# Attention weights times V: one 128-column load of V's two halves in place of two 64-column loads

## What is computed

```python
def _layer(x, wqkv, qs, ksc, wo, lg, lb, w1, b1, w2, b2):
    q, k, v = split(shift_token(x) @ wqkv, 3)          # to 8 heads of 64
    q, k = rotary_xpos(l2norm(q) * qs, l2norm(k) * ksc)
    sim = einsum('bhwid,bhwjd->bhwij', 8 * q, look_around(k))
    attn = softmax(where(mask, -big, sim))
    o = einsum('bhwij,bhwjd->bhwid', attn, look_around(v))
    x = x + o @ wo
    h = layernorm(shift_token(x)) * lg + lb
    a, g = split(h @ w1 + b1, 2)
    return x + (a * gelu(g)) @ w2 + b2
```

## Time and profile before

| what | value |
|---|---|
| median of 3 executions | 3410.75 us (3410.06 to 3413.91) |
| the profiled execution, its own time | 3413.96 us |
| its span, first to last instruction | 3412.1 us |
| mean granted clock of TensorE | 0.977 |
| TensorE matmuls busy / weight loads busy | 95% / 77% of the span |
| VectorE / ScalarE / GpSimd busy | 52% / 43% / 25% |

### The profile page before, as it was taken

The page is one execution under the profiler, slowest core; times in us unless marked ns, Lnnn a source line. Parts: engine busy times, 40 slices in busy tenths (PEclk is TensorE's granted clock), DMA queues, the critical chain, the costliest instruction groups (busy, mean ns, idle before and its releaser), DMA issues. The chain is left out here.

```text
span 3412.1 us, 53427 instructions
## 1 busy us (share of the span) xinstructions
PE 3227.8 (95%) x19624; PEld 2640.0 (77%) x19624; DVE 1765.4 (52%) x3662; ACT 1461.4 (43%) x2957; POOL 841.7 (25%) x1472
## 2 busy tenths in 40 slices
PE   8986999999996999999995999999996999999999
PEld 7975888888875777888774788888885777777777
DVE  4544666666665334434333666666666433334333
ACT  1114777777772111111112777777775211111111
POOL 0005444544436000000002444544543400000000
PEclk9998999999998999999997999999998999999999
DMA  4222111111114111011113111111112311111110
GB/s 140 81 84 90 63 63 60 57 63 60 56 52 121 62 62 56 26 49 62 60 58 138 50 43 49 63 63 60 57 50 81 90 56 62 62 62 62 62 62 32
DMA packets 166889, 224.21 MB, mean 66 GB/s; under 512 B 25017, under 2 KB 94777, under 8 KB 166377
## 3 DMA queue, kind: packets, MB, share of 16 engines
q1 hardware_dynamic: 148152, 201.91, 17.9%
q10 hardware_dynamic: 18480, 18.88, 1.7%
HBM read 130.55 MB, written 60.83 MB: 56 GB/s over the span
## 5 line engine op out<-in xcount | busy, mean ns | idle before, releaser
L308 PE MATMUL bank<-f_hT_hi,f_w_hi 128*128 128x512 f32 (+1 forms) x1408 | 559.5, 397 | 14.7 <-ACT f_hT_hi L973 14.7
L310 PE MATMUL bank<-f_hT_hi,f_w_lo 128*128 128x512 f32 (+1 forms) x1408 | 557.0, 396 | 0.0
L309 PE MATMUL bank<-f_hT_lo,f_w_hi 128*128 128x512 f32 (+1 forms) x1408 | 556.2, 395 | 0.0
L989 ACT ACTIVATE f_gate<-bank,f_b 128x512 f32<-128x512 f32 (+1 forms) x176 | 121.1, 688 | 1004.2 <-PE bank L310 1004.2
L1304 DVE SCALAR_TENSOR_TENSOR f_uraw<-bank,f_b,f_gate 128x512 f32<-128x512 f32 (+1 forms) x176 | 132.1, 750 | 715.6 <-ACT f_gate L989 715.4
L901 ACT ACTIVATE a_P<-a_S,a_bias 128x384 f32<-128x384 f32 x512 | 311.1, 609 | 245.7 <-DVE a_bias L1155 245.7
L1155 DVE CUSTOM_DVE_ANT_0 a_S<-bank,a_masks,a_q 128x384 f32<-128x384 f32 x512 | 295.2, 613 | 61.6 <-issue 45.3
L308 PEld LDWEIGHTS bank<-f_hT_hi,f_w_hi 128*128 128x128 f32 (+1 forms) x1408 | 260.5, 185 | 79.4 <-ACT f_hT_hi L973 15.4
L308 PE MATMUL bank<-a_PT_hi,a_V_hi 128*64 128x128 f32 x1536 | 305.2, 233 | 16.6 <-DVE a_PT_lo L1165 16.6
L310 PEld LDWEIGHTS bank<-f_hT_hi,f_w_lo 128*128 128x128 f32 (+1 forms) x1408 | 260.9, 185 | 67.5
L309 PEld LDWEIGHTS bank<-f_hT_lo,f_w_hi 128*128 128x128 f32 (+1 forms) x1408 | 261.0, 185 | 66.3
(11 more groups left out here) (166 smaller groups left out, 6959.7 us busy)
## 6 DMA issues: line engine op xcount, KB each, us to landing
a_h<-x_layer_in SPq DMA_DIRECT2D x128, 128.0 KB, 2.2
a_res<-x_layer_in SPq DMA_DIRECT2D x64, 256.0 KB, 2.9
x_after_attention<-out_tiles SPq DMA_DIRECT2D x64, 256.0 KB, 2.0
f_h<-x_after_attention ACTq DMA_DIRECT2D x32, 512.0 KB, 4.2
f_res<-x_after_attention SPq DMA_DIRECT2D x64, 256.0 KB, 3.5
f_x<-in_x SPq DMA_DIRECT2D x64, 256.0 KB, 3.5
x_layer_in<-f_res SPq DMA_DIRECT2D x64, 256.0 KB, 2.9
out<-f_res SPq DMA_DIRECT2D x64, 256.0 KB, 3.0
```

The source lines that it names most:

```text
L308: pe.matmul(dst, w[0], m[0], start=start, stop=False)
L309: pe.matmul(dst, w[0], m[1], start=False, stop=False)
L310: return pe.matmul(dst, w[1], m[0], start=False, stop=stop)
L989: act.activation(f_gate[0:ROWS[m], m % 2, :], bank[pair_of(u, m) + 1][0:ROWS[m], :], ACT.Gelu, bias=f_b1[0:ROWS[m], 1, m:m + 1]).then_inc( ...
```

## The change

The high and the low part of V of each head now lie side by side (`a_V` is one tensor with `[head, part, 64]`), so that 128 columns of weights hold both. `pv` loads them, and moves P high and then P low through: two matmuls per key block and head. Each is loaded anew, so there are 12 loads and 12 matmuls per call. The first 64 rows of bank 4 and 5 then hold the product with V high, the last 64 rows that with V low; the two halves have to be added. This now includes the product of both low parts. ScalarE copies one half (`o_half`), VectorE adds the other (`o_add`) into the new tensor `a_O`, and from it `o_hi` and `o_lo` make the two parts of `a_OT` with one 128-row instruction each, in later places of their streams. `pv(x, 0)` now waits for `a_O_added` in place of `a_O_lo`. The carrying DMAs and the zeroing move the same bytes by parts.

```diff
-            a_V = pair(s, "a_V", [P, SLOTS, INNER])
+            a_V = s("a_V", [P, SLOTS, H, 2, HD], F32R)
+            a_O = s("a_O", [P, PAIRS, P])
+            a_O_half = s("a_O_half", [P, PAIRS, P])
...
                     for part in range(2):
-                        keys, values = a_KT[part][:].bitcast(F32), a_V[part][:].bitcast(F32)
+                        keys, values = a_KT[part][:].bitcast(F32), a_V[:].bitcast(F32)
-                        sp.dma_start(values[:, 0:2, :], values[:, QUAD:SLOTS, :]).then_inc(a_carried, 16)
+                        sp.dma_start(values[:, part, :, :, :], values[:, QUAD + part, :, :, :]).then_inc(a_carried, 16)
...
                 def project_out(x):
-                    pe.wait_ge(a_O_hi, START + 2 * (G + x + 1))
-                    pe.wait_ge(a_O_lo, START + 2 * (G + x + 1))
+                    pe.wait_ge(a_O_hi, START + G + x + 1)
+                    pe.wait_ge(a_O_lo, START + G + x + 1)
...
-                        pe.wait_ge(a_O_lo, START + (G + x) * 2)
+                        pe.wait_ge(a_O_added, START + (G + x) * 2)
...
                     for odd in range(2):
-                        h = 2 * i + odd
                         for kb in range(WIN):
-                            mm = three_passes(pe, bank[4 + odd][0:HD, i * P:(i + 1) * P],
-                                              [a_V[n][:, x % QUAD + kb, h * HD:(h + 1) * HD] for n in range(2)],
-                                              [a_PT[n][:, odd, kb * P:(kb + 1) * P] for n in range(2)],
-                                              kb == 0, kb == WIN - 1)
+                            for part in range(2):
+                                mm = pe.matmul(bank[4 + odd][:, i * P:(i + 1) * P],
+                                               a_V[:, x % QUAD + kb, 2 * i + odd, :, :].rearrange("p c d -> p (c d)"),
+                                               a_PT[part][:, odd, kb * P:(kb + 1) * P],
+                                               start=(kb == 0 and part == 0), stop=(kb == WIN - 1 and part == 1))
...
+                def o_half(x):
+                    act.wait_ge(a_PV_mm, START + (G + x + 1) * PAIRS)
+                    act.wait_ge(a_O_added, START + 2 * (G + x))
+                    for odd in range(2):
+                        other, own = slice(HD - odd * HD, P - odd * HD), slice(odd * HD, odd * HD + HD)
+                        act.activation(a_O_half[own, :, :], quarters(bank[4 + odd][other, :]), ACT.Copy).then_inc(a_O_copied, 1)
 
                 def o_hi(x):
-                    act.wait_ge(a_PV_mm, START + (G + x + 1) * PAIRS)
-                    for odd in range(2):
-                        act.activation(a_OT[0][odd * HD:odd * HD + HD, :, :], quarters(bank[4 + odd][0:HD, :]), ACT.Copy)\
-                           .then_inc(a_O_hi, 1)
+                    act.wait_ge(a_O_added, START + 2 * (G + x + 1))
+                    act.activation(a_OT[0][:], a_O[:], ACT.Copy).then_inc(a_O_hi, 1)
...
-                def o_lo(x):
+                def o_add(x):
+                    dve.wait_ge(a_O_hi, START + G + x)
+                    dve.wait_ge(a_O_lo, START + G + x)
                     for odd in range(2):
                         r = slice(odd * HD, odd * HD + HD)
-                        dve.wait_ge(a_O_hi, START + 2 * (G + x) + odd + 1)
-                        dve.tensor_tensor(a_OT[1][r, :, :], quarters(bank[4 + odd][0:HD, :]), a_OT[0][r, :, :], ALU.subtract)\
-                           .then_inc(a_O_lo, 1)
+                        dve.wait_ge(a_O_copied, START + 2 * (G + x) + odd + 1)
+                        dve.tensor_tensor(a_O[r, :, :], quarters(bank[4 + odd][r, :]), a_O_half[r, :, :], ALU.add)\
+                           .then_inc(a_O_added, 1)
+
+                def o_lo(x):
+                    dve.wait_ge(a_O_hi, START + G + x + 1)
+                    dve.wait_ge(a_O_added, START + 2 * (G + x + 1))
+                    dve.tensor_tensor(a_OT[1][:], a_O[:], a_OT[0][:], ALU.subtract).then_inc(a_O_lo, 1)
```

More of the change, by code:

```diff
@@ L235, in adaln_ffn_program @@
         a_PT_mm = sem("a_PT_mm"); a_PT_hi = sem("a_PT_hi"); a_PT_lo = sem("a_PT_lo")
-        a_PV_mm = sem("a_PV_mm"); a_O_hi = sem("a_O_hi"); a_O_lo = sem("a_O_lo")
+        a_PV_mm = sem("a_PV_mm"); a_O_copied = sem("a_O_copied"); a_O_added = sem("a_O_added"); a_O_hi = sem("a_O_hi"); a_O_lo = sem("a_O_lo")
         a_wo_mm = sem("a_wo_mm"); a_out_set = sem("a_out_set"); a_stored = [sem(f"a_stored{i}") for i in range(2)]
@@ L882, in value @@
                     act.wait_ge(a_v_mm, START + G + x + 1)
-                    act.activation(a_V[0][:, x % QUAD + WIN - 1, :], work[:], ACT.Copy).then_inc(a_V_hi, 1)
+                    act.activation(a_V[:, x % QUAD + WIN - 1, :, 0, :], work[:].rearrange("p (h d) -> p h d", h=H), ACT.Copy).then_inc(a_V_hi, 1)
+                def o_half(x):
[4 more added lines that the diff above has]
+                        act.activation(a_O_half[own, :, :], quarters(bank[4 + odd][other, :]), ACT.Copy).then_inc(a_O_copied, 1)
                 def o_hi(x):
-                    act.wait_ge(a_PV_mm, START + (G + x + 1) * PAIRS)
-                    for odd in range(2):
-                        act.activation(a_OT[0][odd * HD:odd * HD + HD, :, :], quarters(bank[4 + odd][0:HD, :]), ACT.Copy)\
-                           .then_inc(a_O_hi, 1)
+                    act.wait_ge(a_O_added, START + 2 * (G + x + 1))
+                    act.activation(a_OT[0][:], a_O[:], ACT.Copy).then_inc(a_O_hi, 1)
                 def normalize(x, i):
@@ L923, in attention @@
                     if here(t - 1):
-                        o_hi(t - 1)
+                        o_half(t - 1)
                     if here(t):
@@ L928, in attention @@
                         normalize(t, 1)
+                    if here(t - 1):
+                        o_hi(t - 1)
                     if here(t + 1):
@@ L1141, in value @@
                     dve.wait_ge(a_V_hi, START + G + x + 1)
-                    dve.tensor_tensor(a_V[1][:, slot, :], work[:], a_V[0][:, slot, :], ALU.subtract).then_inc(a_V_lo, 1)
+                    dve.tensor_tensor(a_V[:, slot, :, 1, :], work[:].rearrange("p (h d) -> p h d", h=H), a_V[:, slot, :, 0, :], ALU.subtract).then_inc(a_V_lo, 1)
                 def mask_max(x, h):
@@ L1196, in attention @@
                     if here(t - 1):
-                        o_lo(t - 1)
+                        o_add(t - 1)
                     if here(t):
@@ L1202, in attention @@
                         mask_max(t, 5)
+                    if here(t - 1):
+                        o_lo(t - 1)
                     if here(t + 1):
@@ L1424, in attention @@
                     pool.memset(a_KT[part][:].bitcast(F32)[:, :, 0:2 * P], 0.0).then_inc(a_carry_zero, 1)
-                    pool.memset(a_V[part][:].bitcast(F32)[:, 0:2, :], 0.0).then_inc(a_carry_zero, 1)
+                    pool.memset(a_V[:].bitcast(F32)[:, part, :, :, :], 0.0).then_inc(a_carry_zero, 1)
                 pool.wait_ge(a_rope_set, START + l + 1)
```

## The result

The changed kernel takes **3506.7 us** (median of 4, 3505.71 to 3510.27), the kernel before 3410.4 us beside it (4 executions, 3409.8 to 3413.91). The ratio is 1.0282, 95% interval 1.0269 to 1.0295: 2.8% slower, against 3503 predicted.

A forecast was written before the change was run, and what follows sets the result against it. TensorE was taken to bound the attention, with no idle time there, so added work adds time. Longer pv calls 67, project_out wait 20, layer ends 3 and 2 make 92 us: 3503 us from the 3410.75 median, range 3465 to 3535.

The forecast's parts named there:

- The load sets the pace and costs 0.11: In pv, 128-column loads start 0.11 us apart, adding 0.26 us per call over 256 calls: 67 us.
- The wait before the projection: Before project_out, TensorE waits 0.34 us more for V's low part, pushed back by o_lo, in 60 steps: 20 us.
- The new copies and the additions cost nothing else: On ScalarE and VectorE, o_half and o_add replace old o_hi and o_lo at no cost; nothing new late in the step's other half.
- The ends: At the layers' ends, 3 us for a longer bare chain plus 2 us for pv calls at half clock.
- The bare chain: Copy, subtraction, projection behind each layer's last tile: 1.5 us longer by a copy and a subtraction, twice, 3 us.
- The steps: In steady attention, TensorE's step was to become 1.38 us longer.
- the sum without the wait: Rival at project_out: the wait for V's low part doesn't grow, leaving 67 + 5, 3483 us; 15%.
- The loads at 0.12: Rival in pv: load and matmul disturb each other, 0.38 us more per call, 3526 us; 13%.
- the overlap at 0.085: Rival in pv: load and matmul overlap better, halfway between 0.06 and 0.11, 3442 us; 5%.
- the quick load: Rival in pv: 128-column load as quick as 64-column, matmul binds at 0.06; 3396, or 3342 without wait growth; 5% together.
- the fall of the clock: Rival in pv: granted clock falls, each call at half clock costing 2 us more; 4%, with anything else unseen.
- fourth rival: The same as the quick load: loads at 0.06 in pv, 3396 us, faster than before; 5% together with 3342.

The follow-up runs named there:

- e2: Changed kernel, but pv loads only the 64 columns of V's high part, still 12 loads and matmuls, V's low part left out of O; 3422.07 us, ratio 1.0028.
- e3: Changed kernel with 128-column loads, but pv moves only 64 of each block's 128 queries, so half of O is missing; 3514.19 us, ratio 1.0298.
- e1: Changed kernel with O's split moved earlier: o_hi ahead of normalize(t,1) on ScalarE, o_lo ahead of mask_max(t,4) on VectorE; 3488.32 us, ratio 1.0215.
- e5: Kernel before the change plus one unused 128x512 subtraction on VectorE ahead of V's low part, pv untouched; 3451.87 us, ratio 1.0116.
- e4: Changed kernel with P high and low moved as one 256-column matmul per load, 6 loads per pv call, sums left out; 3425.41 us, ratio 1.0036.
- e6: e4 with O's split in e1's early places, O still incomplete; 3388.75 us, ratio 0.9930.
- f0: Complete version on e4's matmuls, sums by halves of a tile, O's split as in e1, V's low part after both masked maxima; 3459.54 us, ratio 1.0137.
- f1: f0 with V's low part moved up between the two masked maxima of pair 2; 3503.92 us, ratio 1.0269.
- g1: f0 with the copy and additions of the first two head pairs moved behind K's split of the next tile; 3437.32 us, ratio 1.0073.
- g3: g1 with ScalarE's copy of the last two pairs before exp(t,2) and TensorE's h_T(t+3) transposes before pv(t,2), complete; 3392.49 us, ratio 0.9941.

## Why the prediction was right

- *The load sets the pace and costs 0.11.* Predicted 0.26 per call and 67 us, measured 0.25 and 256 x 0.25 = 64. The row that decided it was that of two loads from idle; e2 and e3 show that it is the load's width and not what moves. What the prediction left open stays open: whether load or matmul sets the 0.06 of the earlier trace rows, since no run moved 64 columns behind a 64-column load.
- *The wait before the projection.* Predicted 0.34 more in 60 steps, 20 us; measured 0.35, and 23.2 - 1.6 = 21.6. e1 takes it away, e5 makes it alone, with the 0.60 that the working used.
- *The new copies and the additions cost nothing else.* e1's step is 1.00 above the one before, four calls of 0.25. Nothing else is left in it.
- *The ends.* The sum has 3 and 2 us for them, and its other terms hold 16 of the 256 calls, 4 us, and 2 of the 60 waits, 1 us, that lie there: 10, against 10.0 measured. The bare chain is 3.0 longer, as predicted: `PE <- ACT a_OT_hi` is 7.3 after, and 4.3 before. What failed is "two `pv` calls per layer run at a granted clock of 0.50". By their loads, 0.107 or 0.213 apart, two run wholly at it in the first layer's end and one in the second's before the change, three and none after it. So the first layer's end took 7.7 more and the second's 2.3, where the sum has 5 for each; that the two misses cancel is luck. The calls' own price was right, in the first layer's end: loads 0.21 apart,

```profile
1055.42 0.33 PEld L686 LDWEIGHTS bank<-a_PT_hi,a_V 128*128 128x128 f32 x1
1055.63 0.33 PEld L686 LDWEIGHTS bank<-a_PT_lo,a_V 128*128 128x128 f32 x1
```

- *The steps.* The 31 steps per layer hold 240 of the calls and 58 of the waits and were to grow by 240 x 0.26 + 58 x 0.34 = 82; they grew by 80. The 29 steady ones per layer grew by 1.38 each, as was said in advance. The first step of a layer has no `pv` call and changed all the same, from 23.92 to 22.76 in the first layer and from 22.84 to 23.09 in the second, for which no cause was looked for. The second grew by 0.40 and 0.52 and not by the 1.00 of its four calls: TensorE waits there in three places, and the waits got shorter.

Of the rivals, the sum without the wait (3483) is refuted by the 21.6 us, and close to what e1 gave, 3488, which is the change without it. The loads at 0.12, the overlap at 0.085 and the quick load are refuted by 0.112, and the fall of the clock by the 1.00 granted from 331 to 1000 us.

Neither rule that the prediction cites shows here. The Trainium skill, "TensorE: Matmul & The Clock Gate", section "Back-to-back issue gap", gives about 81 ns per matmul in a stream of loads and matmuls with 128 moving columns; at full clock it is 0.112 us here with 128-column loads, 0.109 in the transposes, and 0.060 with 64-column loads. The Trainium skill, "TensorE: Matmul & The Clock Gate", section "Weight-path perf modes", has a fast weight load that is on for 128 weights of a type other than FP32; the 128 float32r columns here take 0.112, as long as the transposes' fp32 ones and twice the 0.060 of 64 columns.

The prediction's mechanism has one gap that only the experiments showed. It says what more work on TensorE costs in steady state, and here that was additive: 4 x 0.25 and 0.35 make the 1.38 to 0.03. Less work isn't. Its fourth rival reckoned 3396, faster than before, for loads at 0.06; e2 has such loads, its calls save 0.36 and not 0.28, and it took 3422, slower than before. Each of the kernels that took work from TensorE (e2, e4, e6, f0, f1, g1 to g3) lost more than half of the 88 to 92 us to waits on the other two.

## What to carry to other kernels

Count the columns loaded against the columns moved. Where a float32r weight load here was as wide as what moved through it, 128 and 128, the load was the price, 0.112 us; 12 such matmuls cost more than 18 with 64-column loads, and doubling what moves behind each load took 0.117. To find a wait of a few tenths of a us behind TensorE, measure distances between load starts, not the list of waits. And when an engine stops being the limit, the order of the others' streams decides how much of the gain the time shows, 67 us between f0 and g3 with the same instructions: check who stands behind each piece that is added to a "half idle" engine.

## What the runs showed that I had not expected

The granted clock at a layer's end varies between kernels that issue nearly the same stream. e3 and the changed kernel differ only in how many columns `pv` moves and in two fills of a bank at each layer's start, their steps agree to 0.01 us, and the first layer's end is 55.7 and 55.8 us. The second's is 57.0 and 49.1. The window of e3:

```profile
2666.00:2723.00 57.00, 45.54 (x235) 38.23 (x234) 25.53 (x56) 28.95 (x62) 6.37 (x18) 0.71 0.20 61
```

It stood at 0.90 in the changed kernel. In both profiles TensorE is busy for about 1.75 of the 4 us between 2678 and 2682, at clock 1.00; then the clock falls to 0.63 in e3's next 4 us and to 0.50 for the 12 after them, while the changed kernel keeps 1.00 for 4 more, drops to 0.59 for 4, and stands at 0.99 in the 8 after them. That is 7.8 us in a profiled span, 0.2%. All of the difference between the spans of e3 and of the change (8.4 us) is there but 0.6. It varies between executions of one kernel too: e1's four took 3481.57 us at a mean granted clock of 0.973 and 3489.93 to 3491.01 at 0.970, with 3486.71 at 0.972 between them. So where stretches of a kernel are thinly filled, a change elsewhere can be credited or charged with several us that it has no part in; what decides it was not looked into.
